# Graph attention over 4096 rows: in each step the product with the values comes first, the scores second

## The chip, the cores and the metric

One core of one Trainium2 chip. The time is the device time of one execution in microseconds (us). TensorE (PE) multiplies, VectorE (DVE) and ScalarE (ACT) work elementwise, GpSimd (POOL) does small things, and the SP queue issues nearly all DMAs.

## The reference, cut to what matters

N = 4096 rows, D = 512, all in fp32; adj is a 4096 x 4096 matrix of zeros and ones.

```
h = relu(layernorm(x))
q = h @ Wq.T + bq;  k = key @ Wk.T + bk;  v = value @ Wv.T + bv
s = (q @ k.T) / 64 * adj
s = where(|s| < 1e-5, -1e9, s)
out = x + (softmax(s) @ v) @ Wm.T + bm
```

## The kernel before

The weights are folded at the start: A is made of Wq and Wk, B of Wv and Wm, so that the keys and values themselves, each split into a high and a low fp16 half, stay in SBUF (Kbuf, Vbuf). A product of two split operands takes three matmuls of 128x128 by 128x512 (split_product, lines 470 to 472): high by high, high by low, low by high.

The rows are worked off in 32 blocks b of 128, the 4096 keys in 8 chunks c of 512. A **step** t = 8b + c does one chunk of one block, but in stages that lie many steps apart:

- TensorE: the scores S(t) of this chunk into one of two PSUM banks (lines 608 to 623, 12 matmuls, it waits for z1_ready of step t-2).
- VectorE: z = (S + constant) * adj from PSUM to Zbuf (line 990, it frees the bank), then the masked maximum of the chunk of step t-1 (line 999), then the low half of the probabilities P(u) of tile u = t - 9 (LAG_P, line 1015), then the mask of this step (line 1024). ScalarE takes |z| (line 763), the exp of the block before (line 769, at even c), and the high half of P(u) (line 757).
- SP queue: it waits for z1_ready and loads the chunk of adj for step t+2 (line 341), then waits for the low half (p_lo, line 375) and for the product with the values of tile u-2 (pv_done, line 377), since pT has two buffers, and issues the transpose of P(u) into pT (line 379).
- TensorE: the product with the values PV(u) of tile u = t - 11 (LAG_V, lines 629 to 642, 12 matmuls into O, it waits for pT_in).

Some steps of a block do more. At c = 0 VectorE finds the maximum of the block of rows (lines 1004 to 1008) and the statistics of a coming block (line 799). At c = 1 it normalises that block (line 806) and splits it (line 1060: h). At c = 2 SP transposes h into ho (line 387), behind the transpose of P of that step. At c = 3 TensorE multiplies ho with A (project_q, lines 482 to 496: 8 small matmuls on line 490 and 12 large ones into M1), VectorE splits O (line 1056) and scales q (row_scales, row_units, lines 809 to 840). At c = 4 SP transposes the split O (line 394), at c = 5 the split q (line 400). At c = 6 TensorE multiplies with B (lines 645 to 654, the output product), and VectorE adds the residual (line 1073).

Each engine has its own order written out by hand, and all run through the same steps. Two passes of 16 steps are written out, the middle is a loop, then follow a last pass and 16 steps with what is left. In the first 15 steps or so the keys and values are also still being converted. In TensorE's step the scores stand first, then the product with the values, then project_q or the output product.

Of the kernel before, what the change touches and what calls it, by code (L numbers as in the profile page):

```python
# [25 lines left out]
def adjacency_attention(nc, x, adj, key, value, Wq, bq, Wk, bk, Wv, bv, Wm, bm, out):  # L26
# [15 lines left out]
    CM = CW // P  # L42
    NC = M // CW
# [5 lines left out]
    LAG_V = 11  # L49
# [10 lines left out]
    with ctx:  # L60
        def sb(name, shape, dt=fp32):
            return ctx.enter_context(nc.sbuf_tensor(name, shape, dt))

        def sem(name):
            return ctx.enter_context(nc.semaphore(name))
# [13 lines left out]
        pT = sb("pT", [P, 2, 2, CM, P], fp16)  # L79
# [31 lines left out]
        def bank(name):  # L111
            return ctx.enter_context(nc.psum_tensor(name, [P, 512], fp32))
# [3 lines left out]
        O = [bank("O0"), bank("O1")]  # L116
# [35 lines left out]
        def reads(n, by_act):  # L152

            return sum(read_by_act(k) == by_act for k in range(n + 1))

        def last_fill(what):
            return max(n for n, f in enumerate(FILLS) if f == what)
# [13 lines left out]
        def k_pair(g, half, s):  # L171
            at = (g * 2 + half) * ND * CW + s * CW
            return Kbuf[:, :].bitcast(fp16)[:, at:at + CW]
# [9 lines left out]
        def v_pair(j, half):  # L183
            at = (2 * j + half) * D
            return Vbuf[:, :].bitcast(fp16)[:, at:at + D]
# [5 lines left out]
        def blk(ap, s):  # L191
            return ap[:, s * P:(s + 1) * P]
# [42 lines left out]
        o_hi, o_split, o_in = sem("o_hi"), sem("o_split"), sem("o_in")  # L235
# [18 lines left out]
        pT_in = [sem(f"pT_in{s}") for s in range(2)]  # L254
        p_hi = sem("p_hi")
        p_lo = sem("p_lo")
        pv_done = sem("pv_done")
# [11 lines left out]
        def wait(eng, s, v):  # L269

            if not (isinstance(v, int) and v <= 0):
                eng.wait_ge(s, v)
# [25 lines left out]
        def by_pool(j):  # L298

            return j % 4 == 3 and j > 3  # L300

        def in_pairs(eng, j):

            n = sum(by_pool(k) == by_pool(j) for k in range(j + 1))
            eng.wait_ge(v_ready2 if by_pool(j) else v_ready, n)
# [161 lines left out]
        def _(pe):  # L467
            def split_product(ps, lhs, rhs, start, stop):

                nc.tensor.matmul(ps, lhs[0], rhs[0], start=start, stop=False)  # L470
                nc.tensor.matmul(ps, lhs[0], rhs[1], start=False, stop=False)  # L471
                return nc.tensor.matmul(ps, lhs[1], rhs[0], start=False, stop=stop)  # L472
# [9 lines left out]
            def project_q(n, out_before):  # L482

                if isinstance(n, int) and n == 1:
                    pe.wait_ge(hT_ready, 1)
                else:
                    wait(pe, h_in, 16 * (n - 1))
                for h in range(2):
                    for s in range(ND):
                        nc.tensor.matmul(M0[:, 0:2], ho[:, h, s, :], wpair[:, s, :],  # L490
                                         start=(h == 0 and s == 0), stop=(h == 1 and s == ND - 1))
                wait(pe, res_ready, out_before)
                for s in range(ND):
                    last = split_product(M1[:, :], [ho[:, h, s, :] for h in range(2)],
                                         [A_sb[:, h, s, :] for h in range(2)], s == 0, s == ND - 1)
                last.then_inc(qp_done, 1)
# [8 lines left out]
            def flat_max(what, part, cols):  # L505

                n, bank = TOPS[what]
                pe.wait_ge(part_max, n)
                for c in range(cols):
                    last = nc.tensor.matmul(bank[0:1, c * P:(c + 1) * P], part[:, c:c + 1], ident[:, :], start=True, stop=True)  # L510
                last.then_inc(flat_done, 1)

            def spread_max(what):

                n, bank = TOPS[what]
                pe.wait_ge(top_ready, n)
                nc.tensor.matmul(bank[:, 300:301], ones[0:1, :], gmax[0:1, 3:4], start=True, stop=True).then_inc(top_all, 1)
# [18 lines left out]
            for k in range(ND):  # L536
                pe.wait_ge(w_in[k], 32)
                for s in range(ND):
                    last = nc.tensor.matmul(START[s][:, :], Wq_sb[:, k, s * P:(s + 1) * P], Wk_sb[:, k, :],  # L539
                                            start=(k == 0), stop=(k == ND - 1))  # L540
# [6 lines left out]
            for k in range(ND):  # L547
                last = nc.tensor.matmul(S[0][:, :], bqrep[:, k, :], Wk_sb[:, k, :], start=(k == 0), stop=(k == ND - 1))
            last.then_inc(aside_mm, 1)
            for s in range(ND + 1):  # L550
                for k in range(ND):
                    lhs = Wq_sb[:, k, s * P:(s + 1) * P] if s < ND else bqrep[:, k, :]
                    last = nc.tensor.matmul(S[1][:, s:s + 1], lhs, bkc[:, k:k + 1], start=(k == 0), stop=(k == ND - 1))
# [5 lines left out]
            for k in range(ND):  # L559
                ps = bank_of_next()  # L560
                for s in range(ND):
                    last = nc.tensor.transpose(blk(ps, s), wmv[:, s, k, :], ident[:, :])
# [20 lines left out]
            def transpose_key(g):  # L583
                pe.wait_ge(k_in[g], 16)
                for s in range(ND):
                    ps = bank_of_next()
                    for m in range(CM):
                        last = nc.tensor.transpose(blk(ps, m), k_stage(g)[:, m, s * P:(s + 1) * P], ident[:, :])
                    filled(last)
# [13 lines left out]
            for k in range(ND):  # L603
                last = nc.tensor.matmul(ps[:, :], bvrep[:, k, :], WmT[:, k, :], start=(k == 0), stop=(k == ND - 1))
            filled(last)

            def step(s):
                if s.has_scores:
                    if s.c == 0:
                        if isinstance(s.t, int) and s.t == 0:  # L610
                            pe.wait_ge(q_ready, 1)
                        wait(pe, q_in, 16 * s.b)
                    if isinstance(s.t, int) and s.t < NC:

                        n = last_fill(s.t)
                        if s.t < len(ASIDE):
                            n = max(n, sorted(ASIDE)[s.t])
                        pe.wait_ge(start_dve, reads(n, False))
                    wait(pe, z1_ready, s.t - 1)
                    for f in range(ND):  # L620
                        last = split_product(S[s.j % 2][:, :], [qT[:, s.p, h, f, :] for h in range(2)],
                                             [k_pair(s.c, h, f) for h in range(2)], f == 0, f == ND - 1)
                    last.then_inc(scores_done, 1)
                if isinstance(s.t, int) and s.t < NC - FIRST_KEYS:
                    transpose_key(s.t + FIRST_KEYS)
                if isinstance(s.t, int) and s.t == V_FIRST:
                    flat_max("V", vst[:, 0:1], 1)
                    spread_max("V")
                if s.has_V:
                    jw = s.j - LAG_V  # L630
                    wait(pe, pT_in[jw % 2], 16 * (s.v_turn + 1))
                    if jw % NC == 0:
                        wait(pe, o_split, s.b - 2)
                    if isinstance(s.t, int) and s.t < LAG_V + NC:
                        for m in range(CM):
                            in_pairs(pe, (s.t - LAG_V) * CM + m)
                    for m in range(CM):
                        tile = (jw % NC) * CM + m
                        last = split_product(O[(jw // NC) % 2][:, :], [pT[:, jw % 2, h, m, :] for h in range(2)],
                                             [v_pair(tile, h) for h in range(2)],  # L640
                                             jw % NC == 0 and m == 0, jw % NC == NC - 1 and m == CM - 1)
                    last.then_inc(pv_done, 1)
                if s.c == 3 and s.has_prep:
                    project_q(s.b + 2, s.b - 2)
                if s.c == 6 and s.has_out:
                    wait(pe, o_in, 16 * (s.b - 1))
                    if s.has_prep:

                        wait(pe, q_small, Q_SMALL * (s.b + 1) + 1)
                    wait(pe, res_ready, s.b - 2)  # L650
                    for f in range(ND):
                        last = split_product(M1[:, :], [ho[:, h, f, :] for h in range(2)],
                                             [B_sb[:, h, f, :] for h in range(2)], f == 0, f == ND - 1)
                    last.then_inc(outp_done, 1)

            run(pe, step)


# [444 lines left out]
```

## Time and profile before

| | before |
|---|---|
| median of 3 runs (lowest, highest) | 1620.76 us (1620.57, 1622.99) |
| the profiled execution, and its span | 1620.2 us, 1618.1 us |
| mean granted clock of TensorE | 0.991 |
| PE busy, matmuls | 1578.5 us (98%), 7464 |
| DVE busy | 986.6 us (61%) |
| ACT busy | 603.8 us (37%) |
| POOL busy | 95.1 us (6%) |
| chain of work that ended last | PE 91%, DVE 5%, DMA 2%, ACT 1%, issue 1% |

Busy time is the sum of an engine's instructions without overlaps, and the span runs from the first instruction to the last. The chain is followed back from the last instruction, at each step to what released it. Matmuls are pipelined: each is shown with 379 ns, but they start 216 ns apart.

### The profile page before, as it was taken

To read this page: it belongs to the slowest core of one execution; us is meant where nothing else is said; L and a number is where in the kernel's file an instruction comes from. 1 tells how busy PE (TensorE), PEld (TensorE's weight loads), DVE (VectorE), ACT (ScalarE), POOL (GpSimd) and SP (SyncE) were. 2 spreads that over 40 slices of the span, in tenths; PEclk is the share of its full clock that TensorE was granted. 3 is DMA by queue.
4 is the path that set the end of the run, shared out by engine and by line. 5 is a ranking of instruction groups with operands and counts; after the bars stand their busy time and mean duration, and the time that the engine had idled before them with its cause. 6 is when DMAs were issued, how large, how long until landed. Compare 5 with 4: busy or idle time off the path is not lost.

```text
span 1618.1 us, 23651 instructions
## 1 busy us (share of the span) xinstructions
PE 1578.5 (98%) x7464; PEld 725.7 (45%) x7464; DVE 986.6 (61%) x2238; ACT 603.8 (37%) x975; POOL 95.1 (6%) x155
## 2 busy tenths in 40 slices
PE   8888899999999999999999999999999999999997
PEld 4543344444444444444444444444444444444442
DVE  4788765656666566566666666666565566656541
ACT  2676433333333333333333333333333333333331
POOL 0003100000000000000000000000000000000000
PEclk9999999999999999999999999999999999999999
DMA  9624455565554655555555555555555555555543
GB/s 349 216 66 91 111 118 137 118 124 122 130 117 117 136 119 125 119 123 123 120 126 130 123 117 122 127 120 117 136 117 126 123 127 117 117 135 121 120 101 82
DMA packets 431199, 205.72 MB, mean 127 GB/s; under 512 B 376128, under 2 KB 376128, under 8 KB 431040
## 3 DMA queue, kind: packets, MB, share of 16 engines
q1 hardware_dynamic: 430592, 205.07, 53.4%
q8 instruction: 16, 0.26, 0.1%
q10 hardware_dynamic: 576, 0.27, 0.1%
q14 instruction: 15, 0.12, 0.0%
HBM read 105.13 MB, written 8.39 MB: 70 GB/s over the span
## 4 chain that ended last, share of the span: by engine, by line
PE 91%; DVE 5%; DMA 2%; ACT 1%; issue 1%; SPq 0%; POOL 0%; DVEq 0%; ACTq 0%
PE O L470 13%; PE O L472 13%; PE O L471 13%; PE S L470 13%; PE S L471 13%; PE S L472 13%; PE M L470 3%; PE M L472 3%; PE M L471 3%; DVE Kbuf L894 1%; DMA pT<-ph 1%; DMA ho<-row 1%; DVE Zbuf L990 1%; PE W L539 1%; DVE Zbuf L999 1%
## 5 line engine op out<-in xcount | busy, mean ns | idle before, releaser
L763 ACT ACTIVATE drop<-Zbuf 128x512 f32<-128x512 f32 x256 | 161.4, 631 | 807.6 <-DVE cmx L999 807.6
L990 DVE SCALAR_TENSOR_TENSOR Zbuf<-S,rs,adjb 128x512 f32<-128x512 f32 x256 | 192.0, 750 | 359.9 <-PE S L472 359.1
L470 PE MATMUL O<-Vbuf,pT 128*128 128x512 f16 x1024 | 388.2, 379 | 4.4 <-DMA pT<-ph 4.3
L470 PE MATMUL S<-Kbuf,qT 128*128 128x512 f16 x1024 | 389.1, 380 | 2.8 <-DMA qT<-row 1.5
L472 PE MATMUL S<-Kbuf,qT 128*128 128x512 f16 x1024 | 388.9, 380 | 0.0
L471 PE MATMUL S<-Kbuf,qT 128*128 128x512 f16 x1024 | 388.8, 380 | 0.0
L471 PE MATMUL O<-Vbuf,pT 128*128 128x512 f16 x1024 | 388.1, 379 | 0.0
L472 PE MATMUL O<-Vbuf,pT 128*128 128x512 f16 x1024 | 388.1, 379 | 0.0
L999 DVE CUSTOM_DVE_ANT_0 Zbuf<-drop,Zbuf 128x512 f32<-128x512 f32 x256 | 175.9, 687 | 0.0
L1024 DVE TENSOR_SCALAR drop<-drop,rs 128x512 f32<-128x512 f32 x256 | 143.2, 559 | 35.0 <-ACT drop L763 34.4
L470 PEld LDWEIGHTS O<-Vbuf,pT 128*128 128x128 f16 x1024 | 100.2, 98 | 128.3 <-DMA pT<-ph 7.4
L769 ACT ACTIVATE Zbuf<-Zbuf,smx 128x1024 f32<-128x1024 f32 x128 | 157.0, 1226 | 1.3 <-DVE smx L1008 1.3
L470 PEld LDWEIGHTS S<-Kbuf,qT 128*128 128x128 f16 x1024 | 100.5, 98 | 124.6 <-DMA qT<-row 2.0
L472 PEld LDWEIGHTS S<-Kbuf,qT 128*128 128x128 f16 x1024 | 100.4, 98 | 121.4 <-issue 1.0
L471 PEld LDWEIGHTS S<-Kbuf,qT 128*128 128x128 f16 x1024 | 100.5, 98 | 120.9 <-issue 1.7
L472 PEld LDWEIGHTS O<-Vbuf,pT 128*128 128x128 f16 x1024 | 100.2, 98 | 120.8
L471 PEld LDWEIGHTS O<-Vbuf,pT 128*128 128x128 f16 x1024 | 100.2, 98 | 119.7
L1015 DVE SCALAR_TENSOR_TENSOR ph<-Zbuf,ph 128x512 f16<-128x512 f32 x132 | 91.2, 691 | 9.9 <-ACT ph L757 9.9
L757 ACT ACTIVATE ph<-Zbuf 128x512 f16<-128x512 f32 x132 | 83.0, 629 | 22.2 <-DMA pT<-ph 9.8
L1015 DVE SCALAR_TENSOR_TENSOR osb<-Zbuf,osb 128x512 f16<-128x512 f32 x124 | 84.9, 685 | 3.9 <-ACT osb L757 3.9
L757 ACT ACTIVATE osb<-Zbuf 128x512 f16<-128x512 f32 x124 | 76.2, 615 | 6.2 <-DMA pT<-osb 6.2
L432 POOL TENSOR_TENSOR rstd<-mv,fixed 128x1 f32<-128x1 f32 x32 | 6.1, 190 | 1203.6 <-DVE mv L802 1203.6
(196 smaller groups left out, 1180.3 us busy)
## 6 DMA issues: line engine op xcount, KB each, us to landing
adjb<-in_adj_dram SPq DMA_DIRECT2D x256, 256.0 KB, 2.8
xq<-in_x_dram SPq DMA_DIRECT2D x32, 256.0 KB, 2.8
xr<-in_x_dram SPq DMA_DIRECT2D x32, 256.0 KB, 2.7
out_dram<-xr SPq DMA_DIRECT2D x32, 256.0 KB, 2.3
Kbuf<-in_L_gnn_key_dram SPq DMA_DIRECT2D x7, 1024.0 KB, 14.9
Vbuf<-in_L_gnn_value_dram SPq DMA_DIRECT2D x7, 1024.0 KB, 13.5
pT<-ph SPq DMA_TRANSPOSE x132, 3.1
pT<-osb SPq DMA_TRANSPOSE x124, 3.1
```

What stands on the lines that cost most here:

```text
L470: nc.tensor.matmul(ps, lhs[0], rhs[0], start=start, stop=False)
L471: nc.tensor.matmul(ps, lhs[0], rhs[1], start=False, stop=False)
L472: return nc.tensor.matmul(ps, lhs[1], rhs[0], start=False, stop=stop)
L539: last = nc.tensor.matmul(START[s][:, :], Wq_sb[:, k, s * P:(s + 1) * P], Wk_sb[:, k, :], start=(k == 0), stop=(k == ND - 1))
L757: nc.scalar.activation(rows_p(s)[:, 0, :], probs_of(u), ACT.Copy, scale=PSCALE).then_inc(p_hi, 1)
L763: nc.scalar.activation(drop[:, :], Zbuf[:, s.p, s.c * CW:(s.c + 1) * CW], ACT.Abs).then_inc(abs_ready, 1)
L769: nc.scalar.activation(at, at, ACT.Exp, bias=smx[:, pp, 1:2], scale=smx[:, pp, 2:3], accum_out=psums[:, pp, k:k + 1]).then_inc(exp_done, 1)
L894: nc.vector.scalar_tensor_tensor(out=low, in0=bank_of(fill)[:, :], scalar=scale, in1=high, op0=ALU.mult, op1=ALU.subtract).then_inc(start_ ...
L990: nc.vector.scalar_tensor_tensor(out=z, in0=S[s.j % 2][:, :], scalar=rs[:, r, 3:4], in1=adjb[:, s.j % ADJ_SLOTS, :], op0=ALU.add, op1=ALU. ...
L999: nc.vector.tensor_tensor_reduce(out=last, in0=drop[:, :], in1=last, scale=1.0, scalar=-3.4e38, op0=ALU.add, op1=ALU.max, accum_out=cmx[:, ...
L1015: nc.vector.scalar_tensor_tensor(out=rows_p(s)[:, 1, :], in0=probs_of(u), scalar=PSCALE, in1=rows_p(s)[:, 0, :], op0=ALU.mult, op1=ALU.sub ...
L1024: nc.vector.tensor_scalar(drop[:, :], drop[:, :], rs[:, r, 1:2], rs[:, r, 2:3], ALU.is_lt, ALU.mult)\
```

## The change

In TensorE's step the block for the product with the values moves ahead of the block for the scores. Its waits (pT_in, o_split, and at the start those for the values) move with it. project_q and the output product keep their place at the end of the step, so they now stand behind the scores. Nothing is changed on another engine.

```diff
             def step(s):
+                if s.has_V:
+                    jw = s.j - LAG_V
+                    wait(pe, pT_in[jw % 2], 16 * (s.v_turn + 1))
+                    if jw % NC == 0:
+                        wait(pe, o_split, s.b - 2)
...
+                    for m in range(CM):
+                        tile = (jw % NC) * CM + m
+                        last = split_product(O[(jw // NC) % 2][:, :], [pT[:, jw % 2, h, m, :] for h in range(2)],
...
+                    last.then_inc(pv_done, 1)
                 if s.has_scores:
...
                 if isinstance(s.t, int) and s.t == V_FIRST:
                     flat_max("V", vst[:, 0:1], 1)
                     spread_max("V")
-                if s.has_V:
-                    jw = s.j - LAG_V
-                    wait(pe, pT_in[jw % 2], 16 * (s.v_turn + 1))
...
-                    last.then_inc(pv_done, 1)
                 if s.c == 3 and s.has_prep:
                     project_q(s.b + 2, s.b - 2)
```

**Which product follows a product of scores.** TensorE, behind the scores of step 14 (c = 6 of the second block); O0 and S0 are banks, pT_in0 and pT_in1 announce the transposes of even and odd tiles. Before:

```order
L470 MATMUL S0<-Kbuf,qT 128x512
L471 MATMUL S0<-Kbuf,qT 128x512
L472 MATMUL S0<-Kbuf,qT 128x512
L470 MATMUL O0<-Vbuf,pT 128x512 [waits v_ready,v_ready2,pT_in1]
L471 MATMUL O0<-Vbuf,pT 128x512
L472 MATMUL O0<-Vbuf,pT 128x512
```

The same place of TensorE's order with the change:

```order
L470 MATMUL S0<-Kbuf,qT 128x512
L471 MATMUL S0<-Kbuf,qT 128x512
L472 MATMUL S0<-Kbuf,qT 128x512
L470 MATMUL O0<-Vbuf,pT 128x512 [waits v_ready,v_ready2,pT_in0]
L471 MATMUL O0<-Vbuf,pT 128x512
L472 MATMUL O0<-Vbuf,pT 128x512
```

Scores and values alternate in both. What moved is the tile: behind S(14) stood the product of tile 3, and now that of tile 4 stands there, which is tile t-10 and not t-11.

**What stands before project_q.** TensorE at c = 3. Before:

```order
L470 MATMUL O0<-Vbuf,pT 128x512
L471 MATMUL O0<-Vbuf,pT 128x512
L472 MATMUL O0<-Vbuf,pT 128x512
L490 MATMUL M0<-wpair,ho 128x2 [waits h_in]
L490 MATMUL M0<-wpair,ho 128x2 x7
L470 MATMUL M1<-A_sb,ho 128x512 [waits res_ready]
```

And with the change:

```order
L470 MATMUL S1<-Kbuf,qT 128x512
L471 MATMUL S1<-Kbuf,qT 128x512
L472 MATMUL S1<-Kbuf,qT 128x512
L490 MATMUL M0<-wpair,ho 128x2 [waits h_in]
L490 MATMUL M0<-wpair,ho 128x2 x7
L470 MATMUL M1<-A_sb,ho 128x512 [waits res_ready]
```

project_q now follows the scores of its step directly, and a product with values stands behind it.

## Rows read from the trace of the kernel before

**Rows 1.** Table by stretches: busy us of PE, PEld, DVE, ACT, POOL; granted clock; DMA.

```profile
100.00:200.00 100.00, 82.43 (x368) 35.57 (x367) 77.10 (x163) 56.97 (x94) 23.73 (x22) 0.93 0.40 94
...
700.00:900.00 200.00, 200.00 (x964) 91.22 (x963) 124.38 (x291) 69.48 (x114) 9.12 (x16) 1.00 0.53 122
...
1570.00:1580.00 10.00, 8.33 (x39) 3.33 (x38) 3.10 (x8) 4.26 (x7) 1.35 (x1) 1.00 0.69 138
```

**Rows 2.** Timeline of TensorE, one block: start us, us, line, out<-in.

```profile
792.10 0.38 PE L470 MATMUL S<-Kbuf,qT 128*128 128x512 f16 x1
...
794.69 0.38 PE L470 MATMUL O<-Vbuf,pT 128*128 128x512 f16 x1
...
797.28 0.34 PE L490 MATMUL M<-wpair,ho 128*128 128x2 f16 x8
...
800.07 0.38 PE L470 MATMUL S<-Kbuf,qT 128*128 128x512 f16 x1
...
807.84 0.38 PE L470 MATMUL O<-Vbuf,pT 128*128 128x512 f16 x1
...
825.97 0.38 PE L470 MATMUL O<-Vbuf,pT 128*128 128x512 f16 x1
```

**Rows 3.** Timeline of VectorE, the same block.

```profile
784.53 0.75 DVE L990 SCALAR_TENSOR_TENSOR Zbuf<-S,rs,adjb 128x512 f32<-128x512 f32 x1 [1.45 <-PE S L472]
...
789.30 0.69 DVE L1060 SCALAR_TENSOR_TENSOR row<-xq,row 128x512 f16<-128x512 f32 x1 [0.69 <-ACT row L777]
...
808.04 0.75 DVE L990 SCALAR_TENSOR_TENSOR Zbuf<-S,rs,adjb 128x512 f32<-128x512 f32 x1 [1.87 <-PE S L472]
...
809.32 0.69 DVE L1015 SCALAR_TENSOR_TENSOR ph<-Zbuf,ph 128x512 f16<-128x512 f32 x1
...
826.44 0.75 DVE L990 SCALAR_TENSOR_TENSOR Zbuf<-S,rs,adjb 128x512 f32<-128x512 f32 x1 [2.79 <-PE S L472]
...
828.76 0.68 DVE L1015 SCALAR_TENSOR_TENSOR osb<-Zbuf,osb 128x512 f16<-128x512 f32 x1
```

**Rows 4.** Timelines of VectorE and the SP queue at c = 4 of another block.

```profile
477.10 0.69 DVE L1015 SCALAR_TENSOR_TENSOR osb<-Zbuf,osb 128x512 f16<-128x512 f32 x1
...
476.74 0.35 SPq L341 DMA_DIRECT2D adjb<-in_adj_dram  x1
477.96 1.25 SPq L379 DMA_TRANSPOSE pT<-osb  x1
```

**Rows 5.** Timelines at the end of the kernel: VectorE, SP queue, TensorE.

```profile
1567.32 0.75 DVE L990 SCALAR_TENSOR_TENSOR Zbuf<-S,rs,adjb 128x512 f32<-128x512 f32 x1 [1.84 <-PE S L472]
...
1569.97 1.23 SPq L379 DMA_TRANSPOSE pT<-ph  x1
...
1573.05 0.39 PE L470 MATMUL O<-Vbuf,pT 128*128 128x512 f16 x1 [0.59 <-DMA pT<-ph]
```

**Rows 6.** Timelines of the SP queue and TensorE at c = 2 and 3.

```profile
277.62 1.24 SPq L379 DMA_TRANSPOSE pT<-osb  x1
279.13 1.25 SPq L387 DMA_TRANSPOSE ho<-row  x1
...
282.25 0.35 PE L490 MATMUL M<-wpair,ho 128*128 128x2 f16 x8
```

**Rows 7.** Totals of waits: who <- for whom: us, times, longest.

```profile
PEld M L490 <- DMA ho<-row: 11.6, 7, 6.5
...
PE O L470 <- DMA pT<-ph: 4.3, 6, 1.2
...
SPq L378 <- PE O L472: 86.1, 176, 1.4
```

**Rows 8.** Line 379, the transpose issued at 477.96 alone.

```profile
DMA to landing us min/median/max: 3.5/3.5/3.5
```

**Rows 9.** Timeline of TensorE at the start, after a long wait.

```profile
186.88 0.35 PE L490 MATMUL M<-wpair,ho 128*128 128x2 f16 x8 [3.59 <-DMA ho<-row]
...
191.10 0.63 PE L470 MATMUL S<-Kbuf,qT 128*128 128x512 f16 x1
```

More of the change, by code:

```diff
@@ L607, in step @@
             def step(s):
+                if s.has_V:
[3 more added lines that the diff above has]
+                        wait(pe, o_split, s.b - 2)
+                    if isinstance(s.t, int) and s.t < LAG_V + NC:
+                        for m in range(CM):
+                            in_pairs(pe, (s.t - LAG_V) * CM + m)
+                    for m in range(CM):
+                        tile = (jw % NC) * CM + m
+                        last = split_product(O[(jw // NC) % 2][:, :], [pT[:, jw % 2, h, m, :] for h in range(2)],
+                                             [v_pair(tile, h) for h in range(2)],
+                                             jw % NC == 0 and m == 0, jw % NC == NC - 1 and m == CM - 1)
+                    last.then_inc(pv_done, 1)
                 if s.has_scores:
@@ L628, in step @@
                     spread_max("V")
-                if s.has_V:
-                    jw = s.j - LAG_V
-                    wait(pe, pT_in[jw % 2], 16 * (s.v_turn + 1))
[L632 to L641, printed above, removed]
-                    last.then_inc(pv_done, 1)
                 if s.c == 3 and s.has_prep:
```

## The prediction

> **What bounds the kernel now.** I read the table by stretches first, then TensorE's timeline over one block of rows, then the totals of waits, and last the timelines of VectorE and the SP queue around the transposes. In the stretch 700 to 900 us TensorE is busy for all of its 200 us at a granted clock of 1.00, VectorE for 124 us [rows 1]. So TensorE is the bound, with no hole in it: an order of the same matmuls can win nothing there, and each wait that it opens is paid in full.
>
> I write S(t) for the score product of step t, PV(u) for the product with the values of tile u, c for t modulo 8, and e for the end of an S, taken as the start of the next group. A group of 12 matmuls takes 2.59 us (792.10 to 794.69), project_q 2.79 (797.28 to 800.07) [rows 2]. So a step is 5.18 us, and a block of 8 steps with project_q and the output product 46.8.
>
> The reader is to see in the rows how much room PV and project_q have. VectorE starts on S(5) 0.20 after its end (807.84 is the start of the next group, 808.04 that of L990) and has the low half of P(t-9) done 1.97 later (809.32 + 0.69 - 808.04) [rows 2, 3]. The transpose starts 0.17 behind a low half (477.10 + 0.69 to 477.96) if nothing else holds it [rows 4]. From its start to the matmul that waits for it are 3.08 us (1569.97 to 1573.05) [rows 5]. That is 5.42 us from e. Before the change four groups lie between the end of S(t) and PV(t-9), 10.36 us, so none of this shows. What nearly shows is project_q at c = 3: it needs the transpose of h, which SP issues at c = 2 behind that step's P transpose, 1.51 later (277.62 to 279.13), and 3.12 more pass until its first matmul (282.25) [rows 6]. PEld waited for this transpose in 7 of the blocks [rows 7]: the chain is already nearly as long as its cover.
>
> **The change, part by part.** No instruction is added or removed on any engine; VectorE, ScalarE and SP keep their order. TensorE's order S(t), PV(t-11) becomes PV(t-11), S(t). In the row this means that PV(t-10) and not PV(t-11) follows S(t): each PV comes one group earlier against the scores. But VectorE and SP still work P(t-9) off behind S(t). project_q and the output product stay behind the second group of their step, which is now S.
>
> 1. The room of a P transpose, from the end of S(t) to the start of PV(t-9), falls from 10.36 to 5.18 us: PV(t-10) and S(t+1). Only where project_q or the output product lies between (c = 2, 3, 5, 6) is it 7.8 to 8.0, and nothing waits.
>
> 2. The chain in a plain step. SP waited for PV two tiles back before most transposes (L378, 176 times) [rows 7]. That PV is now done first, so the transpose starts 0.17 after the low half and only 1.22 us after the load of adj was issued. At c = 4 this spacing exists already (476.74, 477.96) [rows 4], and that transpose landed in 3.5 us instead of 3.08 [rows 8]. I take that nearest row, plus 0.04 to the matmul: 0.20 + 1.97 + 0.17 + 3.54 = 5.88. Over 5.18 this is **0.70 us at c = 7 and at c = 4**. The other end is 3.08: 5.42, a wait of 0.24. At c = 1 the wait of point 3 has already moved S(2) back, and nothing is left.
>
> 3. At c = 0 VectorE has the row's maximum and bn_stats ahead of the low half: 3.00 us (826.44 to 828.76 + 0.68), and starts 0.47 after e (825.97) [rows 2, 3]. This transpose is further from adj, so 3.08: 0.47 + 3.00 + 0.17 + 3.08 = 6.72. S(1) ends 5.88 after S(0) by then, so **0.84** more.
>
> 4. project_q at c = 3 follows S(3) directly. From the end of S(2) to it lie PV and S(3), 5.18 us; before, another PV, 7.77. Its chain from the end of S(2): 0.20 + 1.97 + 0.17 + 1.51 + 3.12 = 6.97 [rows 3, 4, 6]. VectorE is free for it: its c = 1 work ends 5.46 after it began (784.53 to 789.30 + 0.69) [rows 3], and S(2) now ends about 6.0 after S(1). So **1.79 us**. It hides nothing of the others, since PV and S(4) follow and their chains shift along. Behind it row_scales on VectorE starts no later than now, because the split of O holds VectorE until then anyway.
>
> 5. The output product at c = 6 has 10 us from S(4) to its operand, transposed at c = 4, which needs 7. Nothing. The q transpose has two steps. Nothing.
>
> 6. The start. TensorE is busy for only 82.43 of the 100 us to 200 [rows 1]: VectorE and ScalarE convert the values beside the steps and set the pace. Behind the first project_q PV(1) now comes before S(12), so VectorE gets S(12) a group later. I charge that group, 2.6 (from 0, if their slack absorbs it, to 4, if a second one adds).
>
> 7. The end. S(255) now has one PV more ahead of it and one fewer behind it: 2.59 later. The first transpose of the tail no longer waits for PV: it starts at 1567.32 + 1.97 + 0.17 = 1569.46 instead of 1569.97, 0.5 back [rows 5]. Net 2.1 (0 to 3).
>
> Sum: 30 blocks x 0.70 (c = 4) = 21.0; 29 x (0.70 + 0.84) (c = 7, 0) = 44.7; 28 blocks with a project_q x 1.79 = 50.1; start and end 4.7. Together 120.5, on the profiled execution's 1620.2 us, which stands 0.6 under the median of the runs: **1741 us**, 7.4% slower.
>
> For points 2 to 4 the rows give 3.08 to 3.5 us from a transpose's start to its landing [rows 5, 8]. The Trainium skill, "DMA: Bandwidth & Descriptors", section "Anatomy of one DMA", fits about 2.0 us plus the bytes over 436 GB/s for a DMA on GpSimd's path; for the 256 KB of two halves (128 x 2 x 512 in two bytes) that is an estimate of 2.6 us. By it point 2 would vanish and the sum be near 1696. The trace does not agree.
>
> Lower bound: 3.08 for every landing and 0.20 for the start at c = 0: 0.24 x 30 + (0.24 + 1.03) x 29 + 1.79 x 28 = 94, nothing at start and end: 1714. Upper bound: VectorE starts 0.47 late everywhere, every transpose takes the 3.5 of the close one: about 0.97 x 30 + (0.97 + 1.03) x 29 + 2.4 x 28 = 154, and 7 for start and end: 1781.
>
> **The rivals.**
> - *The clock falls too.* The new wait before project_q is 1.8 us in each block. After one of 3.59 us the product's 2.79 us became 4.22 (186.88 to 191.10), and the next matmul still takes 0.63 instead of 0.38, the 1.2 GHz level [rows 9]. Against it: the stretch 1570 to 1580 has holes (8.33 busy of 10) and a granted clock of 1.00 [rows 1]. If it came, 28 x 1.43 = 40 us more: 1781. The Trainium skill, "TensorE: Matmul & The Clock Gate", Part 1, has idleness throttle the array by half; by that rule this rival holds only if 1.8 us is idleness enough, which no row here shows.
> - *Only project_q waits.* If landings stay near 3.0 and VectorE answers at once, PV hardly waits: 28 x 1.79 and c = 0 alone, 29 x 1.2, 85 us, and 2 for the end: 1707. For it: the median landings; against it: the close-spaced one.
> - *Faster.* The mechanism is the freed SP queue: it waits no more for the PV two tiles back, so its transposes start up to 0.5 us earlier, at the end of the kernel too. If the chains of points 2 and 4 fit into 5.18 us, TensorE stays full, and the gain is at most the 4.3 us that it waited for P transposes [rows 7]: 1616. It decides only if a landing takes under 2.8 us and the h transpose under 1.3; every row is above that.
> - *Nothing changes*, because the two orders are one alternation and VectorE's slack absorbs the shift: 1620. Against it: the waits lie on latency, which idle time of an engine doesn't shorten.
>
> **How the numbers follow.** My forecast 0.76, the clock 0.09, project_q alone 0.09, nothing 0.03, faster 0.03. The range takes in both bounds and the first rival, and opens a little below the second: 1698 to 1788. A measurement of this kernel tells 0.2% (3 us) from no change. Faster 0.03, same 0.03, slower 0.94.
>
> **What would show it.** In the profile after: PEld L490 <- DMA ho<-row in some 28 waits of about 1.8 us; PE O L470 <- DMA pT in three waits per block, 0.7 to 0.9 each; SP's wait for PV (L378) gone; a block of 50.8 us instead of 46.8; PE's clock still 1.00; VectorE's and ScalarE's times of one unchanged. I am wrong if project_q doesn't wait, if the PV waits at c = 7, 0 and 4 are missing or above 1.2 us, or if matmuls of 0.63 us appear in every block.

## The result, and the profile after

The changed kernel takes 1754.92 us (median of 4 runs, 1754.7 to 1755.72), the kernel before 1621.18 beside it: a ratio of 1.083 (95% interval 1.081 to 1.084). The profiled execution took 1754.7 us against 1620.2, so there are 134.5 us to account for. Forecast were 1741, 120.5 us more.

The page of the changed kernel: span, busy time of the engines, the chain that ended last by engine and by line.

```profile
span 1752.6 us, 23651 instructions
...
PE 1603.7 (92%) x7464; PEld 717.3 (41%) x7464; DVE 984.8 (56%) x2238; ACT 600.7 (34%) x975; POOL 94.3 (5%) x155
...
PE 59%; DMA 19%; DVE 14%; issue 3%; SPq 2%; ACT 1%; DVEq 0%; POOL 0%; ACTq 0%
DMA pT<-osb 11%; PE O L470 9%; PE O L472 8%; PE O L471 8%; PE S L472 7%; PE S L470 7%; PE S L471 7%; DMA ho<-row 5%; DVE Zbuf L999 4%; DVE Zbuf L990 3%; PE M L470 3%; PE M L472 3%; PE M L471 3%; DVE osb L1015 3%; SPq L379 2%
```

No engine has more work: the instructions are the same 7464 matmuls. PE's busy time is 25 us longer than before (1603.7 for 1578.5) mostly because the last 0.16 us of a matmul as drawn, which the next one normally covers, count as busy at each wait. TensorE is busy for 92% and not 98% of the span, and the chain that ended last, which was TensorE for 91%, now runs through DMA for 19% and VectorE for 14%. The DMAs in it are the transposes pT<-osb and ho<-row.

The totals of waits, TensorE's and then the SP queue's (answers to [rows 7]):

```profile
PEld M L490 <- DMA ho<-row: 72.3, 30, 2.7
...
PE M L490 <- DMA ho<-row: 57.6, 30, 2.2
PE O L470 <- DMA pT<-osb: 44.2, 60, 1.5
...
PE O L470 <- DMA pT<-ph: 21.0, 35, 2.8
...
SPq L378 <- PE O L472: 10.2, 8, 2.8
```

The h transpose was waited for in 7 blocks and now in all; P transposes, 6 waits before, have 95; SP's wait for PV (L378) fell from 176 times to 8. The table by stretches (answers to [rows 1]; PE, PEld, DVE, ACT, POOL, then clock):

```profile
100.00:200.00 100.00, 82.68 (x363) 35.09 (x362) 76.71 (x162) 55.14 (x92) 23.90 (x22) 0.93 0.38 88
700.00:900.00 200.00, 184.86 (x865) 81.49 (x866) 111.41 (x258) 62.22 (x103) 8.87 (x16) 0.99 0.50 112
```

In 700 to 900 TensorE is busy for 184.86 us, not 200. In 100 to 200 nothing is lost (82.68, before 82.43). TensorE's timeline of one block, the first matmul of five groups, with the idle time before it:

```profile
709.92 0.38 PE L470 MATMUL O<-Vbuf,pT 128*128 128x512 f16 x1
...
716.02 0.39 PE L470 MATMUL O<-Vbuf,pT 128*128 128x512 f16 x1 [0.76 <-DMA pT<-osb]
...
734.59 0.39 PE L470 MATMUL O<-Vbuf,pT 128*128 128x512 f16 x1 [0.27 <-DMA pT<-ph]
...
740.82 0.39 PE L470 MATMUL O<-Vbuf,pT 128*128 128x512 f16 x1 [0.88 <-DMA pT<-osb]
...
753.18 0.35 PE L490 MATMUL M<-wpair,ho 128*128 128x2 f16 x8 [1.83 <-DMA ho<-row]
```

709.92 follows S(4). Then stand the wait before PV behind S(5), those behind S(0) and S(1), and project_q. A block takes 51.3 us on average (S(21) to S(255) in 1499.4 us), before 46.8; the prediction had 50.8. The idle time is measured from the drawn end of the last matmul, 0.16 us after the next could have started; so 0.76 is a loss of 0.92 us. Below, a loss is the time between the starts of two groups less a group's own.

The chain of the first of these waits, on VectorE and the SP queue, answers to [rows 3, 4]:

```profile
710.37 0.75 DVE L990 SCALAR_TENSOR_TENSOR Zbuf<-S,rs,adjb 128x512 f32<-128x512 f32 x1 [2.15 <-PE S L472]
...
711.64 0.69 DVE L1015 SCALAR_TENSOR_TENSOR osb<-Zbuf,osb 128x512 f16<-128x512 f32 x1
...
711.28 0.35 SPq L341 DMA_DIRECT2D adjb<-in_adj_dram  x1
712.50 1.25 SPq L379 DMA_TRANSPOSE pT<-osb  x1
```

z starts 0.45 after e (709.92 to 710.37), the low half ends 1.96 later, the transpose starts 0.17 behind it, 1.22 behind the load of adj. Its landing, answer to [rows 8]:

```profile
DMA to landing us min/median/max: 3.5/3.5/3.5
```

From 712.50 to the matmul at 716.02 are 3.52. The whole chain is 6.10 us in a room of 5.18, and 0.92 is what TensorE lost.

The chain before project_q, VectorE at c = 2 and the SP queue:

```profile
746.42 0.75 DVE L990 SCALAR_TENSOR_TENSOR Zbuf<-S,rs,adjb 128x512 f32<-128x512 f32 x1 [0.98 <-PE S L472]
...
748.55 1.25 SPq L379 DMA_TRANSPOSE pT<-osb  x1
749.99 1.27 SPq L387 DMA_TRANSPOSE ho<-row  x1
```

S(2) ended at 746.01 (its PV follows there). z starts 0.41 later, P's transpose at 748.55, that of h 1.44 behind it, project_q 3.19 after that, at 753.18: 7.17 in a room of 5.18.

### The profile page after: what moved, and what is told of

Read it like the earlier page. It is cut to its first block, busy times and chain, and to the rows that moved or that the text cites. A ratio compares the mean times of both kernels' runs of the same rounds, so it can differ in the third digit from the quotient of the medians.

```text
span 1752.6 us, 23651 instructions
## 1 busy us (share of the span) xinstructions
PE 1603.7 (92%) x7464; PEld 717.3 (41%) x7464; DVE 984.8 (56%) x2238; ACT 600.7 (34%) x975; POOL 94.3 (5%) x155
## 4 chain that ended last, share of the span: by engine, by line
PE 59%; DMA 19%; DVE 14%; issue 3%; SPq 2%; ACT 1%; DVEq 0%; POOL 0%; ACTq 0%
DMA pT<-osb 11%; PE O L470 9%; PE O L472 8%; PE O L471 8%; PE S L472 7%; PE S L470 7%; PE S L471 7%; DMA ho<-row 5%; DVE Zbuf L999 4%; DVE Zbuf L990 3%; PE M L470 3%; PE M L472 3%; PE M L471 3%; DVE osb L1015 3%; SPq L379 2%
## 5 line engine op out<-in xcount | busy, mean ns | idle before, releaser
L1024 DVE TENSOR_SCALAR drop<-drop,rs 128x512 f32<-128x512 f32 x256 | 164.6, 643 | 35.0 <-ACT drop L763 34.8
```

What stands on the lines that cost most here:

```text
L1024: nc.vector.tensor_scalar(drop[:, :], drop[:, :], rs[:, r, 1:2], rs[:, r, 2:3], ALU.is_lt, ALU.mult)\
```

## The experiments

Each kernel was timed against the kernel before on one chip, where that took 1621.0 us (median). In brackets stands the ratio to it, with its 95% interval. A balance of parts goes by the one execution that was profiled, which can be some 2 us off the median.

**e1: project_q a group later, in the changed kernel.**

```diff
+                if s.c == 4 and s.has_prep:
+                    project_q(s.b + 2, s.b - 2)
                 if s.has_scores:
...
-                if s.c == 3 and s.has_prep:
-                    project_q(s.b + 2, s.b - 2)
```

> The changed order, but project_q stands a group later, behind PV of step 4 and ahead of S(4), as far behind S(2) as before the change. My theory (each transpose has a chain of fixed length from the end of a product of scores, and what it exceeds its room by is waited for): the wait of 2.1 us before project_q goes, and the PV behind S(3), which had project_q as cover, gets a wait of 0.8 like its neighbours. 28 x (2.2 - 0.8) = 40 us less: about 1715 us. Rival (the wait before project_q only stands in for one that PV would have anyway, so it moves): the PV behind S(3) waits some 2 us and the time stays near 1755.

Measured 1730.1 us (1.067, 1.066 to 1.069). The waits of TensorE:

```profile
PE O L470 <- DMA pT<-osb: 77.2, 87, 1.4
...
PE O L470 <- DMA pT<-ph: 26.1, 38, 3.1
```

No wait for ho is left, and PV behind S(3) loses 0.79 on average, as expected. But PV behind S(5) rose from 0.79 to 1.29. VectorE and TensorE there:

```profile
752.59 0.14 DVE L840 TENSOR_SCALAR rs<-rs 128x1 f32<-128x1 f32 x1
752.70 0.75 DVE L990 SCALAR_TENSOR_TENSOR Zbuf<-S,rs,adjb 128x512 f32<-128x512 f32 x1
...
751.85 0.38 PE L470 MATMUL O<-Vbuf,pT 128*128 128x512 f16 x1
...
758.33 0.39 PE L470 MATMUL O<-Vbuf,pT 128*128 128x512 f16 x1 [1.14 <-DMA pT<-osb]
```

row_units ends at 752.73 only and z of S(4) starts 0.85 after e (751.85), where it was 0.40 in the changed kernel. The balance over 28 blocks: 62 us less, 22 and 14 more, 26 together, 25 measured. The wait before project_q is a real one and doesn't move; 15 of the 40 us that I expected (62 less 22) are lost because project_q carries VectorE's row_scales with it, which I had not counted.

**e2: PV a whole step later, in the changed kernel.**

```diff
-    LAG_V = 11
+    LAG_V = 12
```

(and LAST = LAG_V + 4). Behind S(t) again stands PV(t-11), project_q stays directly behind S(3).

> The changed order with LAG_V 12 for 11: PV of tile t-12 and then S(t), so that PV(t-11) follows S(t) as before the change; project_q stays directly behind S(3). My theory: no PV waits, project_q waits about 2.1 us in 28 blocks: 1621 + 28 x 2.2 = about 1683 us. Rival (it is the two-buffered pT or the new place of the waits in the step that costs, not the room): it stays near 1755, with PV waits of 0.5 to 1 us.

Measured 1732.2 us (1.068, 1.066 to 1.070), well over the 1683. Waits, the stretch 400 to 1400, and TensorE's timeline at one project_q:

```profile
PE M L490 <- DMA ho<-row: 77.2, 30, 9.0
...
PE O L470 <- DMA pT<-ph: 3.2, 4, 1.3
```

```profile
400.00:1400.00 1000.00, 957.80 (x4434) 427.70 (x4432) 566.46 (x1297) 325.35 (x535) 45.26 (x80) 0.97 0.49 114
```

```profile
897.46 0.35 PE L490 MATMUL M<-wpair,ho 128*128 128x2 f16 x8 [2.45 <-DMA ho<-row]
...
898.24 0.63 PE L472 MATMUL M<-A_sb,ho 128*128 128x512 f16 x1
```

The P waits are gone: 4 in all. So the room decides, neither pT nor the place of the wait in the step: SP waits for PV two tiles back again (L378, 206 times, in the changed kernel 8), and it costs PV nothing. That wait does cost project_q something: at c = 2 it starts P's transpose, and with it that of h, 2.91 us after the end of S(2) and not 2.61, so project_q loses 2.4 us and not 2.1. The granted clock is 0.97. After the wait of 2.45 the matmuls of the product are drawn with 0.63, the 1.2 GHz level. In 23 of 28 blocks the product and what follows took 1.7 us longer: 66 us of waits and 39 of slow matmuls, with 6 us at the start and 2 at the end, make up the 113 of the profiled execution (1733.2). This is the rival on the clock, which in the changed kernel came in 2 of 28 blocks.

**e3: e1 and e2 together.**

> Both edits: LAG_V 12 and project_q behind PV of step 4. TensorE's order is then that of the kernel before, except that the output product stands a group earlier. My theory: 1621 us, within 3 us of the kernel before, and no wait in the blocks. Rival (something else than the room, such as the clock or the instruction stream of the new step): clearly over 1621, up to 1690.

Measured 1623.1 us (1.0012, 1.0002 to 1.0021). The stretch 400 to 1400:

```profile
400.00:1400.00 1000.00, 1000.00 (x4784) 455.33 (x4782) 613.62 (x1409) 351.51 (x576) 49.88 (x88) 1.00 0.54 124
```

TensorE is busy for the whole 1000 us. With the old distances, in the new place of the code, nothing of the 134 us remains but some 2.

**e5: the load of adj behind the transposes of its step, in the changed kernel.**

```diff
-                if s.has_scores and s.more_adj:
-
-                    wait(sp, z1_ready, s.t + 1)
-                    load_adj(s.b + (s.c + ADJ_SLOTS) // NC, (s.c + ADJ_SLOTS) % NC, s.j % ADJ_SLOTS)
...
                     sp.dma_start_transpose(ho[:, :, :, :].rearrange("p h s n -> p (h s) n"), rows).then_inc(h_in, 16)
+                if s.has_scores and s.more_adj:
+
+                    wait(sp, z1_ready, s.t + 1)
+                    load_adj(s.b + (s.c + ADJ_SLOTS) // NC, (s.c + ADJ_SLOTS) % NC, s.j % ADJ_SLOTS)
```

> The changed kernel, but SP issues the load of adj behind the transposes of P and h of its step instead of ahead of them. My theory (the transposes land in 3.3 to 3.5 us and not in 3.1 because the load of adj started 1.2 us earlier on the same DMA engines): the landing falls to 3.1, the waits of PV at c = 4 and 7 shrink by 0.2 to 0.4 each, about 13 us less in all: 1742 us. Rival (the longer landing comes from the transposes themselves or from what follows them): landing stays 3.3 to 3.5 and the time 1755.

Measured 1748.5 us (1.078, 1.076 to 1.080). Issue to landing on the page:

```profile
pT<-ph SPq DMA_TRANSPOSE x132, 3.1
pT<-osb SPq DMA_TRANSPOSE x124, 3.1
```

3.1 us, where the changed kernel's page has 3.3. The load of adj just ahead does lengthen the transpose: from issue to the matmul are 3.10 us on average at c = 4 and at c = 7, where the changed kernel has 3.44 and 3.34. The losses behind S(0) and S(5) shrank from 0.49 to 0.30 and from 0.79 to 0.46. But behind S(1) it grew from 1.05 to 1.23: that chain counts from S(0), and what the PV ahead of it no longer waits, it waits itself. Five project_q ran slowly and not two. So 6 us and not 13.

**e8: h transposed first in its step, in the changed kernel.** The block of SP's step for c = 2 (line 382 ff.) moves to the head of the step, ahead of load_adj and the P transpose.

> The changed kernel, but at c = 2 SP issues the transpose of h ahead of the load of adj and of the P transpose of that step, so its chain no longer starts at the end of S(2). My theory: the 2.1 us before project_q go whole, with the few slow project_q behind them, and the waits of PV stay as they are: 28 x 2.2 = 62 us less, about 1693 us. Rival (moving project_q's wait lets VectorE's row_scales push S(4) as when project_q stood later): the PV wait behind S(5) grows from 0.8 to 1.3 and about 14 us come back, 1707.

Measured 1690.1 us (1.042, 1.041 to 1.044), 65 us under the changed kernel. SP queue and TensorE:

```profile
721.37 1.23 SPq L375 DMA_TRANSPOSE ho<-row  x1
723.14 0.34 SPq L341 DMA_DIRECT2D adjb<-in_adj_dram  x1
724.35 1.25 SPq L386 DMA_TRANSPOSE pT<-osb  x1
...
726.99 0.34 PE L490 MATMUL M<-wpair,ho 128*128 128x2 f16 x8
```

The transpose of h starts 5.6 us ahead of project_q, which follows its S(3) (724.40) without a wait. The other losses stayed, within 0.05 us (0.53, 1.00 and 0.82 behind S(0), S(1) and S(5)), so the rival, that row_scales would push S(4), did not come. The 65 us are the 62 of project_q and its slow matmuls, and 4 at the start, which the expectation had not counted. One reordering on the DMA queue is worth half of what the change cost.

**e4: the low half ahead of z, in the changed kernel.** VectorE's block "if s.has_P" (line 1012) moves ahead of line 982, and on SP the load of adj moves behind the P transpose.

> The changed kernel, but VectorE does the low half of P(t-9) ahead of the z of its step, and SP issues that transpose ahead of the load of adj. The P chain then no longer starts at the end of S(t), and at c = 2 the transpose of h waits for z1 of the step only and not for the low half. My theory: no PV waits, project_q waits 0 to 0.3 us, total 1625 us (1621 and 2 to 4 at start and end). Rival (PV waits because of something other than where the chain starts, such as the landing or the pT buffers): PV waits of 0.5 us or more remain and the time is over 1670.

Measured 1662.0 us (1.024, 1.023 to 1.026). The losses of PV in the blocks are all zero: the chain of P hung on S(t) only by the order on VectorE. But project_q still loses 1.2 us, so the time is not the 1625 that I expected. The SP queue at c = 2 and TensorE:

```profile
766.88 1.24 SPq L375 DMA_TRANSPOSE pT<-osb  x1
768.51 0.34 SPq L341 DMA_DIRECT2D adjb<-in_adj_dram  x1
769.11 1.24 SPq L387 DMA_TRANSPOSE ho<-row  x1
...
772.52 0.35 PE L490 MATMUL M<-wpair,ho 128*128 128x2 f16 x8 [1.01 <-DMA ho<-row]
```

The P transpose holds the queue for 1.24 us, then the load of adj goes, and h behind it at 769.11, 3.41 before project_q. Not z held the load: z ran from 766.63 for 0.75 us and was done while the P transpose still occupied the queue. I had overlooked that a transpose occupies the queue while it is issued. The other 8 us are at the start: TensorE is busy for 76.6 of 100 to 200. There VectorE waits more for ScalarE than in the kernel before (for the high half 3.9 us in 6 waits against 2.0 in one, for |z| 9.1 against 3.1), with z queued behind the low half. That this is what costs the 8 us is likely but not shown.

**e6: as e4, with the load of adj behind h too.**

> As the kernel with the low half first, but the load of adj also stands behind the transpose of h. My theory: every chain fits its room; within 3 us of the kernel before, 1621 to 1625 us, for the changed order itself then costs only what start and end take. Rival: the same as above, over 1670; or a load of adj that now comes too late for VectorE: waits of L990 for DMA adjb, and the time over 1630.

Measured 1630.8 us (1.0053, 1.0036 to 1.0070). This is over the range that I gave it. project_q loses 0.2 us on average (5 us in all), PV nothing, and z never waits for adj; the rest is 5 us at the start, where TensorE reaches the same work at 201.94 and not at 196.54.

**e10: as e6, but h also ahead of P.**

> The changed order of TensorE with every chain shortened: SP transposes h first in its step, then P, then loads adj, and VectorE does the low half ahead of z. My theory: no waits are left in the blocks, also not the 0.2 us before project_q; what remains over the kernel before is the start, about 5 us, as in the other kernels with the low half first: 1626 us. Rival (the changed order has a cost of its own in the blocks): over 1635.

Measured 1623.4 us (1.0015, 1.0006 to 1.0024). The table by stretches:

```profile
100.00:200.00 100.00, 81.76 (x356) 34.47 (x355) 75.80 (x158) 52.74 (x87) 24.65 (x22) 0.91 0.37 87
400.00:1400.00 1000.00, 1000.00 (x4784) 455.49 (x4783) 602.62 (x1407) 348.01 (x574) 58.87 (x88) 1.00 0.53 123
```

TensorE's new order is as full as the old one when the chains fit its room: from S(21) to S(255) it takes 1368.0 us, in the kernel before 1368.0. The start cost 1 us and not the 5 that I expected.

**e7: the moves of e6 in the kernel before.**

> The same two moves on VectorE and SP in the kernel before, with the scores first. My theory: TensorE was full there already, so nothing changes in the blocks; only start and end can move: 1620 us, within 3. Rival (VectorE's late low halves cost something at the start, where VectorE sets the pace): 1615 or less.

Measured 1626.4 us (1.0028, 1.0017 to 1.0039): 5 us slower, outside the 3 that I gave it, and the other way than the rival had it. The blocks are full. The loss is again at the start (TensorE busy for 77.7 of 100 to 200, before 82.4).

**e11: e2 with h first.**

> The kernel with LAG_V 12 (1732 us, where project_q waited 2.4 us and then nearly always ran slowly) with the one more edit that SP transposes h first in its step. My theory: the slow project_q is a consequence of the wait before it, so both go together: no wait, no matmuls of 0.63 us in the blocks, and 1615 to 1623 us. Rival (the slow clock comes from the order of the products itself): the wait goes, but the slow matmuls stay in most blocks, 28 x 1.7 = 47 us, about 1665.

Measured 1620.5 us (0.9994, 0.9984 to 1.0003), 112 us less than e2. The stretch 400 to 1400:

```profile
400.00:1400.00 1000.00, 1000.00 (x4784) 454.87 (x4782) 612.24 (x1411) 351.51 (x578) 49.88 (x88) 1.00 0.53 123
```

Without the wait no block has a slow product: the slow clock followed the wait, not the order of the products.

**e9: h first, in the kernel before.**

> The kernel before with the one edit that SP transposes h first at c = 2. My theory: the blocks are full and stay so; at the start project_q waits 6.0 and 3.6 us for h and then runs at the lower clock, and h would land about 3 us sooner each time: a gain of 2 to 8 us, 1613 to 1619. Rival (VectorE and ScalarE set the pace of the start, so the time moves into another wait): 1621, within 2.

Measured 1615.1 us (0.9964, 0.9951 to 0.9978), faster than both kernels. TensorE at the first two project_q of the loop, and the stretch 100 to 200:

```profile
131.89 0.35 PE L490 MATMUL M<-wpair,ho 128*128 128x2 f16 x8 [2.17 <-DMA ho<-row]
...
183.92 0.35 PE L490 MATMUL M<-wpair,ho 128*128 128x2 f16 x8
...
100.00:200.00 100.00, 85.64 (x394) 37.31 (x395) 81.02 (x170) 59.68 (x97) 23.77 (x22) 0.97 0.44 101
```

The second project_q starts 2.96 us sooner than in [rows 9] (186.88), without a wait, and no longer runs at the lower clock; the first waits 2.2 us where it waited 6.0. TensorE is busy for 85.64 of the 100 us, 3.2 more. The blocks were full before and are now. That VectorE and ScalarE alone set the pace of the start was wrong.

## Why the prediction was right

The result lies in the range, 14 us above the forecast. What was lost, by the points of the prediction, in the profiled execution (mean loss times blocks):

| step | forecast us | measured us |
|---|---|---|
| PV behind S(5), the c = 4 of point 2 | 0.70 x 30 = 21.0 | 0.79 x 30 = 23.7 |
| PV behind S(0), the c = 7 of point 2 | 0.70 x 29 = 20.3 | 0.49 x 29 = 14.2 |
| PV behind S(1), point 3 | 0.84 x 29 = 24.4 | 1.05 x 29 = 30.5 |
| project_q, point 4 | 1.79 x 28 = 50.1 | 2.09 x 28 = 58.6 |
| slow matmuls after it, the first rival | 0 | 3.4 |
| start, point 6 | 2.6 | 1.1 |
| end, point 7 | 2.1 | 2.0 |
| sum | 120.5 | 133.5 of 134.5 |

- **Point 1**, that each PV comes a group nearer to S, held. e2 and e3 show it: with the distance restored the waits are gone.
- **Point 2** held in kind. At c = 4 the transpose to the matmul took 3.44 us on average for the 3.54 of the close load, and e5 shows that the load causes the length. What I had too small was the start of z: 0.20 from the row of S(5), where at c = 4 it is 0.41. The two errors partly cancel. At c = 7 the start of z was right (0.20) and I had the landing too long: 3.34 to the matmul and not 3.54.
- **Point 3**: its chain, 6.72 from the end of S(0), was right, on average over the blocks. The loss is larger because c = 7 lost less, and the sum of the two is what counts: 1.54 both forecast and measured.
- **Point 4** gave the largest term and was mis-sized by most: 1.79 for 2.09. Its chain is 7.27 us on average and not 6.97: here too z starts 0.4 and not 0.2 after e, and the transpose of h is 0.1 longer. That VectorE is free in time held, and e8 shows that the term stands by itself.
- **Point 5** held: the output product and the q transpose never waited.
- **Point 6** was charged with 2.6 and cost 1.1: at the same amount of work TensorE is at 197.65 instead of 196.54. But not in the way that I gave: S(12) started only 0.2 us later (140.33 for 140.14), although PV(1) stood ahead of it, because the project_q before it ran at full clock and took 2.8 us, where it had taken 5.3 in the kernel before. That this hid the group was luck.
- **Point 7** was right: from the end of S(255) to the end of the span are 50.3 us, before 51.0, with one PV of 2.59 fewer in them.
- **The clock.** In 2 of 28 blocks the product after the wait was slow. This is the place:

```profile
804.73 0.35 PE L490 MATMUL M<-wpair,ho 128*128 128x2 f16 x8 [2.05 <-DMA ho<-row]
...
806.37 0.63 PE L470 MATMUL M<-A_sb,ho 128*128 128x512 f16 x1
```

The Trainium skill's "TensorE: Matmul & The Clock Gate", Part 1, has idleness take the clock down, and the trace agrees in kind.

The fit for GpSimd's path in the Trainium skill's "DMA: Bandwidth & Descriptors", section "Anatomy of one DMA", gave an estimate of 2.6 us for a transpose. The runs show 3.1 alone and 3.3 to 3.5 close behind a load. With 2.6 in its own terms the prediction's sum comes to about 1693, not to the 1696 given there.

Of the 13 us by which the sum was short, 2.7 are behind S(5) (z 0.2 later, less a landing 0.1 shorter), 8.5 before project_q, of which the start of z makes 0.2 x 28 = 5.6, and 3.4 the clock; the start gave 1.5 back. Behind S(0) and S(1) the errors cancel (6.1 us each way), because one chain from the end of S(0) fixes their sum.

## What to carry to other kernels

On a full engine the order of two independent products cost next to nothing by itself here (e10: 1623.4 us against 1621.0); what moves is the distance between a producer and its consumer, in time. Write for each consumer the chain from what it hangs on (also by mere order on another engine's queue) to its start, and compare it with the work that lies between: where the chain is longer, the difference is lost in each turn, and any queue that puts an urgent transfer behind a later need is the first place to shorten it. A kernel whose engine shows no idle time can have a chain that just fits: in the kernel before the transpose of h was issued 4.38 us after the end of S(2) on average, 4.69 at the latest, and takes 3.1 more, in a room of 7.77.

## What the hardware showed that I had not expected

- **The clock after short waits is not settled by their length.** After waits of 2.25 to 2.61 us in e2, 23 of 28 products ran partly at 1.2 GHz; in the changed kernel 2 of 28, after 2.22 and 2.34, while others after 2.34 and 2.35 did not; in e5 5 of 28, two of them after less than 2.0. What decides it is open. The cost of a slow stretch hardly varied: 1.60 to 1.69 us in all three kernels.
- **z starts 0.2 us after the end of an S at some steps and 0.4 at others**, steadily so by step: on average 0.40 to 0.42 at c = 0, 2, 4 and 6 of the changed kernel, 0.20 to 0.28 at the odd ones. No run here tells why; it wasn't tried.
- **A transpose of 256 KB holds the SP queue for 1.25 us** and lands 0.2 to 0.4 us later when a load of 256 KB was issued 1.2 us ahead of it (e5 against the changed kernel).
